# First FFN tile: the gate product moved from VectorE to GpSimd

## What is computed

```
I = gate_up_packed.shape[0] // 2                      # 1408
w_gu = _dequant_fp4(gate_up_packed, gate_up_scales, GROUP_SIZE)
w_down = _dequant_fp4(down_packed, down_scales, GROUP_SIZE)
gate_up = jnp.einsum('bsh,oh->bso', x, w_gu)
gate, up = (gate_up[..., :I], gate_up[..., I:])
h = jax.nn.silu(gate) * up                            # the gate product
y = jnp.einsum('bsi,hi->bsh', h, w_down)
rms = jnp.sqrt(jnp.mean(y * y, axis=-1, keepdims=True) + EPS)
return y / rms
...
x = x + 0.5 * _L0_ffn_ref(_layernorm(x, axis=-1), ...)
x = x + _L0_attn_ref(_layernorm(x, axis=-1), ...)
x = x + 0.5 * _L0_ffn_ref(_layernorm(x, axis=-1), ...)
```

## Time and profile before

| what | value |
|---|---|
| time, median of 3 | 2580.82 us (2577.58 to 2581.5) |
| profiled execution, its own time | 2581.73 us |
| its span | 2579.8 us |
| TensorE busy | 2480.4 us (96%) |
| VectorE busy | 1811.5 us (70%) |
| ScalarE busy | 1460.7 us (57%) |
| GpSimd busy | 1532.8 us (59%) |
| mean granted TensorE clock | 0.995 |

### The profile page before, as it was taken

How to read it: one execution, slowest core, us unless ns; L and a number is a source line. 1 busy time by engine, 2 the same in 40 slices (tenths; PEclk the granted TensorE clock), 3 DMA queues, 4 the chain that set the end, 5 groups by cost and what they waited for, 6 DMA issues and landing times.

```text
span 2579.8 us, 39633 instructions
## 1 busy us (share of the span) xinstructions
PE 2480.4 (96%) x14559; PEld 1099.3 (43%) x14559; DVE 1811.5 (70%) x3100; ACT 1460.7 (57%) x2829; POOL 1532.8 (59%) x1537
## 2 busy tenths in 40 slices
PE   5899999999999999999999999999999999999998
PEld 3444444444443444433344434444333444444443
DVE  7866666678659594948586695858475866666666
ACT  6666666665225656565632255565665466666664
POOL 3466666764325767676342266676774467766775
PEclk9999999999999999999999999999999999999999
DMA  2012211121122020200140221020004301111101
GB/s 67 17 42 77 95 42 50 50 98 50 50 59 61 6 51 10 64 6 3 60 155 33 70 50 44 14 50 25 3 4 154 116 17 50 50 50 50 50 33 49
DMA packets 78017, 130.57 MB, mean 51 GB/s; under 512 B 19552, under 2 KB 24699, under 8 KB 77695
## 3 DMA queue, kind: packets, MB, share of 16 engines
q1 hardware_dynamic: 77822, 128.05, 16.1%
HBM read 68.23 MB, written 31.46 MB: 39 GB/s over the span
## 4 chain that ended last, share of the span: by engine, by line
PE 79%; DVE 7%; ACT 4%; issue 2%; SPq 1%; POOL 1%; DMA 0%; DVEq 0%; ACTq 0%; POOLq 0%
PE pp L97 60%; PE ps L97 18%; ACT sb L103 4%; DVE sb L112 4%; DVE sb L118 1%; SPq L139 1%; POOL sb L106 1%; DVE sb L109 1%; PE ps L100 1%; DVE sb L106 1%; DMA sb<-sb 0%; PE pp L100 0%; DVE sb L115 0%; DVE sb L124 0%; DVE sb L127 0%
## 5 line engine op out<-in xcount | busy, mean ns | idle before, releaser
L97 PE MATMUL pp<-sb,sb 128*128 128x512 f16 (+8 forms) x11230 | 2068.5, 420 | 32.4 <-DVE sb L112 12.8
L106 POOL TENSOR_TENSOR sb<-sb,sb 128x512 f32<-128x512 f32 (+7 forms) x1353 | 1491.1, 1128 | 1019.4 <-ACT sb L103 349.3
L97 PEld LDWEIGHTS pp<-sb,sb 128*128 128x128 f16 (+3 forms) x11230 | 799.5, 102 | 1068.2 <-issue 213.9
L97 PE MATMUL ps<-sb,sb 128*128 128x512 f16 (+8 forms) x2786 | 723.7, 348 | 35.1 <-DVE sb L112 21.6
L103 ACT ACTIVATE sb<-pp 128x512 f32<-128x512 f32 (+6 forms) x1035 | 521.2, 560 | 331.9 <-PE pp L97 317.1
L118 DVE TENSOR_REDUCE sb<-pp 128x1 f32<-128x512 f32 (+3 forms) x704 | 440.3, 665 | 150.2 <-PE pp L97 149.9
L103 ACT ACTIVATE sb<-sb 128x512 f16<-128x512 f32 (+4 forms) x513 | 326.2, 650 | 376.1 <-DVE sb L112 327.7
L112 DVE SCALAR_TENSOR_TENSOR sb<-pp,sb,sb 128x512 f32<-128x512 f32 x447 | 324.0, 745 | 137.8 <-PE pp L97 118.3
L112 DVE SCALAR_TENSOR_TENSOR sb<-ps,sb,sb 128x512 f32<-128x512 f32 x437 | 316.0, 745 | 136.6 <-PE ps L97 113.9
L97 PEld LDWEIGHTS ps<-sb,sb 128*128 128x128 f16 (+3 forms) x2786 | 249.9, 98 | 351.0 <-DVE sb L112 46.4
L103 ACT ACTIVATE sb<-ps 128x512 f32<-128x512 f32 (+5 forms) x473 | 262.8, 567 | 153.5 <-PE ps L97 123.6
(11 more groups left out here) (29 smaller groups left out, 376.8 us busy)
## 6 DMA issues: line engine op xcount, KB each, us to landing
sb<-sb SPq DMA_DIRECT2D x144, 128.0 KB, 2.4
sb<-L_attn_X SPq DMA_DIRECT2D x64, 256.0 KB, 3.6
sb<-xa SPq DMA_DIRECT2D x64, 256.0 KB, 4.2
sb<-xc SPq DMA_DIRECT2D x64, 256.0 KB, 3.4
xa<-sb SPq DMA_DIRECT2D x32, 256.0 KB, 2.0
xc<-sb SPq DMA_DIRECT2D x32, 256.0 KB, 4.3
out<-sb SPq DMA_DIRECT2D x32, 256.0 KB, 2.0
sb<-sb SPq DMA_DIRECT2D x48, 96.0 KB, 2.1
```

The costliest lines, as they stand in the source:

```text
L97: return self.e.matmul(*a, **k) if self.e else self
L106: return self.e.tensor_tensor(*a, **k) if self.e else self
```

## The change

The gate products of chunks 0 to 10 of the first feed-forward are no longer issued by VectorE but by GpSimd, with the same operands, shapes and semaphores. gate_dve goes. A wait that ordered the first product of the second tile behind the last of the first tile goes too, since both are now in one queue.

```
--- before.py
+++ after.py
@@ -748,9 +748,7 @@
                     e.wait_ge(*p.out.stored[q].at((1, 3)))
         elif what == "silu":
             n = at[0]
-            if f.deq and n < IC:
-                gate_dve(e, p, f, n)
-            elif n == NT * IC - 1:
+            if n == NT * IC - 1:
                 e.wait_ge(*f.silu_done.at(n))
                 e.wait_ge(*f.ev_dve.at((NT - 1, IC - 1, 3, 1)))
                 e.wait_ge(*f.h2_made.at(n - 2))
@@ -837,14 +835,6 @@
-def gate_dve(e, p, f, n):
-    e.wait_ge(*f.silu_done.at(n))
-    e.wait_ge(*f.ev_dve.at((n // IC, n % IC, 3, 1)))
-    if n >= 2:
-        e.wait_ge(*f.h2_made.at(n - 2))
-    e.tensor_tensor(p.h[n % 2][:, :], p.sil[n % 2][:, :], p.acc[1][n % 3][:, :], ALU.mult).then_inc(*f.h_made.up(n))
@@ -913,13 +903,11 @@
         elif what == "silu":
             n = at[0]
-            if not (f.deq and n < IC) and n < NT * IC - 1:
+            if n < NT * IC - 1:
                 e.wait_ge(*f.silu_done.at(n))
                 e.wait_ge(*f.ev_dve.at((n // IC, n % IC, 3, 1)))
                 if n >= 2:
                     e.wait_ge(*f.h2_made.at(n - 2))
-                if n == IC:
-                    e.wait_ge(*f.h_made.at(n - 1))
                 e.tensor_tensor(p.h[n % 2][:, :], p.sil[n % 2][:, :], p.acc[1][n % 3][:, :], ALU.mult).then_inc(
                     *f.h_made.up(n))
```

More of the change, by code:

```diff
@@ L839, in roots_pool @@
     yield
[L842 to L847, removed]
 def constants_pool(e, p):
```

## The result

The changed kernel takes 2583.53 us, median of 22 runs (2581.84 to 2586.18), the kernel before 2579.99 us, median of 22 runs (2577.58 to 2581.96). The ratio is 1.0014, with a 95% interval of 1.0008 to 1.0021: 3.5 us slower, between 2.1 and 5.4. The forecast was 3.5 us slower. The difference is less than the 0.2% that was called "same", though with this many runs it stands clear of zero.

What follows compares the result with a forecast made beforehand. Up to 140 us a loop through transpose, GpSimd's six instructions and VectorE's second half was taken as the bound, not VectorE's product. Terms 0.2 + 2.0 + 0.4 + 0 + 0.5 + 0.4 = 3.5 us slower gave 2584.3 us, range 2581.0 to 2589.0.

Steps and rivals of the forecast that it cites:

- The loop: First tile: (3,1), transpose, GpSimd's six, VectorE's second half, (3,1), 9.83 us long; VectorE's product is not in it.
- The size per chunk: Chunks 1 to 4: GpSimd's six start later, 0.36 us from its queue alone to 0.62, taken as 0.5.
- Chunk 0: First chunk, where GpSimd's next work already started late: +0.2 us (0.05 to 0.3).
- Chunk 5: Norm statistics follow the decode, so VectorE gains a little by losing the product: +0.4 us (0.3 to 0.6).
- Chunk 7: Four 128x4 steps follow; the product on GpSimd adds one instruction to wait behind: +0.5 us (0.1 to 0.6).
- Chunks 9 and 10: GpSimd had been idle 5.13 and 5.07 us before its next work, so 0.
- Chunk 8: Small steps right behind the product would wait, with ScalarE's applications on the path: +0.4 us (0.1 to 0.9).
- Chunk 6: GpSimd's next work started late because TensorE had run at half clock; the delay is covered: 0.
- Rival 1, the clock: Longer TensorE waits in chunks 1 to 5 make its clock fall more often, 0.75 us each: 2587.0 us, chance 0.27.
- a clock at 0.50 in chunks 1 to 5: TensorE at 1.2 GHz in those first-tile chunks, named as a sign that the forecast is wrong.
- Rival 2: VectorE is the bound after all; chunks 0 to 8 gain 0.6 us each, 5.4 us faster: 2575.4 us, chance 0.05.
- rival 3: GpSimd's late start is taken up by shorter waits, the loop keeps 9.83 us: 2580.8 us, chance 0.10.

Runs made afterwards that it cites:

- the long write: Kernel before, with GpSimd writing 128x1400 zeros into a spare tile where the change puts its product: 2582.08 against 2580.65 us, ratio 1.0006.
- the first two experiments: Against the kernel before: first-tile products cut to 8 of 512 columns, ratio 0.9990; one more 0.68 us VectorE instruction behind each product, ratio 1.0008.
- the shorter write: Kernel before, with GpSimd writing 128x1152 zeros into a spare tile where the change puts its product: 2580.67 against 2580.29 us, ratio 1.0000.

## Why the prediction was right

**The loop** (transpose, GpSimd's six, VectorE's second half) was read right: taking the product away or adding an instruction on VectorE left it within 0.12 us, while occupying GpSimd for 1.27 us lengthened it by 0.35.

**The size per chunk**, 0.36 to 0.62, taken as 0.5: measured 0.50 (chunk 3) and 0.63 (chunk 1), where the clock did not fall; chunk 1 is just over the upper bound. The lower bound was the queue alone, and that was measured as 0.35. "Which engine goes first looks even": each order occurs four times in the trace. The term for chunks 1 to 4 together, 2.0 with bounds 1.4 and 2.5, does not hold in the profiled execution, where it is 3.36, since the clock fell in two of them.

**Chunk 0**: +0.2 forecast, +0.22 measured. **Chunk 5**: +0.4, measured +0.47. **Chunk 7**: +0.5, measured +0.44, and the reason, one more instruction to wait behind, holds: the small steps come 0.6 us later because the last decode step waits for GpSimd's product (1.44 us). It is the port's doing and not the queue's, since there the kernel with the zero-writing GpSimd was faster than before. **Chunks 9 and 10**: 0, measured 0.

**Chunk 8** was mis-sized: +0.4 forecast, +0.06 measured, just under the lower bound of 0.1. The last of the small steps and (1,0) of the next chunk, before and changed:

```profile
117.14 0.16 DVE L106 TENSOR_TENSOR sb<-sb 128x4 f32<-128x4 f32 x1
117.91 0.75 DVE L112 SCALAR_TENSOR_TENSOR sb<-pp,sb,sb 128x512 f32<-128x512 f32 x1 [0.61 <-PE pp L97]
```

```profile
120.25 0.68 DVE L106 TENSOR_TENSOR sb<-sb 128x4 f32<-128x4 f32 x1
120.85 0.74 DVE L112 SCALAR_TENSOR_TENSOR sb<-pp,sb,sb 128x512 f32<-128x512 f32 x1
```

The product did make them wait, as forecast: they end 0.7 us later after (3,1). But before, VectorE was idle for 0.61 us behind them, and (1,0) starts 2.05 us after (3,1) in both kernels (115.86 and 118.8). The wait fits into that gap because the small steps also start 0.8 us earlier, with VectorE's own product gone from in front of them. In the run with the product on both engines they had it still in front, and there the time behind chunk 8 was 10.07 us instead of 8.24. The prediction left out both, the gap and what the missing product gives back here.

**Chunk 6** was put at 0 because the clock had fallen there. In the changed trace it fell elsewhere, and the chunk took 10.46 us, as chunk 5 did: the term is -0.65 against a disturbed 11.11 and would be near +0.5 against the undisturbed 9.99. The step took an event of one execution for a property of the kernel.

**The sum** is right in part by luck. Measured against an undisturbed chunk 6, the forecast left out 0.47 us, and it put 0.34 too much on chunk 8; the two nearly cancel. In the profiled pair it is the falls in chunks 2 and 4 that weigh against the one in chunk 6.

**Rival 1, the clock**, happened in part: two falls, each making its chunk about 0.6 us longer than an undisturbed one of the changed kernel (10.95 against 10.3 to 10.5), near the 0.75 forecast. Over the runs it did not decide: the median lies 3.5 us above before, the interval's end at 5.4 just below this rival's 6.2. Whether falls are more frequent in the changed kernel on average is not settled, but the mean granted clocks bound it: 0.9951 over the changed kernel's 22 executions, 0.9955 over the 83 of the kernel before that ran beside the experiments, and one fall of 3.4 us is 0.0007 of the span. That is about half a fall more per execution, within the noise and hardly more than one, so the clock may hold 0.3 us of the 3.5. The prediction had named a clock at 0.50 in chunks 1 to 5 as a sign against itself; the sign came, with a cost too small to decide. Waits of 2.49 and 2.36 us came before the two falls, waits of 2.50 and 2.49 us behind chunks 5 and 6 came before none, and in the run with the long write waits of 2.2 to 2.4 us before none.

**Rival 2** fell with the first two experiments, and rival 3 with the loop of 10.2 us in the long write.

Of what was to be seen in the profile, the loop's 10.2 to 10.5 us, the product at 1.27 to 1.52 us right ahead of the scaled pair, TensorE's wait of 2.3 to 2.5 us (1.7 behind the two falls) and nothing behind 140 us are there, the loop with the exception of the two chunks of 10.95. The longer idle time of VectorE is not, or only in part: from 45 to 90 us its busy time fell by 3.0 us and not by the 3.4 of five products, although it issued a tenth fewer other instructions (76 against 85), because part of the new waiting is inside its instructions and counted as busy.

## What to carry to other kernels

An engine that is 92% busy need not be the bound: look behind the instruction that is to be moved for idle time and for what ends it, and look whether neighbours of the same form vary in length (0.24 to 0.79 us here), since waiting for a shared port is counted as busy. Moving work to the emptier engine puts it in front of what is queued there, and if that queue's first entry starts the next round of the loop, each 0.35 us of delay is paid every round. Where two engines alternate on a port, making one of them wait until the other's short steps are through can be worth more (here 6 us) than any split of the work between them.

## What the runs showed that I had not expected

- GpSimd's six instructions and VectorE's four short steps run in lockstep, and one wait on a semaphore undoes it: 2.33 to 0.90 us for the four steps.
- GpSimd's instructions slow even VectorE's 128x4 steps, from 0.15 to about 0.65 us, so a chain of such steps grows up to fourfold when it meets GpSimd's run.
- Delaying GpSimd can speed up VectorE by accident: with the zero-writing instruction the time behind chunk 7 fell from 8.79 to 8.28 us (8.06 with the shorter write), since one or two of the 128x4 steps got through before GpSimd's run began.
- Two products of the same size at the same time, one per engine, cost about twice what one on GpSimd does: the loop grows from 9.83 to 10.91 us, against 10.32 to 10.46.
